# Lead-in of a self-attention: the first pair's queries side by side in both halves, dense products in half steps, fewer filler products

## The reference

```
qkv = x_norm @ W_qkv + b_qkv            # x_norm: layer norm, scaled and shifted
q, k, v = jnp.split(qkv, 3, axis=-1)    # each (B, 1024, 256) -> 16 heads of 16
attn_w = jax.nn.softmax(jnp.einsum('bhqd,bhkd->bhqk', q, k) * scale, axis=-1)
attn_out = jnp.einsum('bhqk,bhkd->bqhd', attn_w, v)
attn_out = attn_out @ W_proj + b_proj
x = x + gate_a[:, None] * attn_out
```

## Time and profile before

| | us |
|---|---|
| median of 3 runs | 1573.97 |
| the runs | 1573.97, 1571.93, 1583.33 |
| the profiled execution | 1573.0 |
| its span | 1571.2 |
| its mean granted PE clock | 0.978 |

### The profile page before, as it was taken

How to read it: one execution, slowest core, us unless ns; L and a number is a source line. 1 busy time by engine, 2 the same in 40 slices (tenths; PEclk the granted TensorE clock), 3 DMA queues, 4 the chain that set the end, 5 groups by cost and what they waited for, 6 DMA issues and landing times.

```text
span 1571.2 us, 26548 instructions
## 1 busy us (share of the span) xinstructions
PE 1452.7 (92%) x10495; PEld 915.3 (58%) x10495; DVE 1052.8 (67%) x2994; ACT 767.8 (49%) x1248; POOL 395.9 (25%) x447
## 2 busy tenths in 40 slices
PE   5889999999999999978998999999999999997898
PEld 3447674344455857656774767444445585765676
DVE  2584356899847446799547544799983754679953
ACT  1335422788844533335552643288884453332554
POOL 4420015642125100113215000664202510001320
PEclk9899998899999999999999999999999999999999
DMA  9500024221020000000040000632102000000000
GB/s 339 174 1 1 0 83 94 42 43 22 2 81 1 1 1 3 2 1 1 1 165 11 1 1 0 165 53 42 22 2 81 1 1 0 3 2 1 1 1 27
DMA packets 41503, 57.86 MB, mean 37 GB/s; under 512 B 10915, under 2 KB 30659, under 8 KB 40603
## 3 DMA queue, kind: packets, MB, share of 16 engines
q1 hardware_dynamic: 25239, 34.71, 6.8%
q0 software_dynamic: 13360, 14.09, 5.1%
q10 hardware_dynamic: 2780, 7.36, 1.3%
HBM read 40.26 MB, written 2.10 MB: 27 GB/s over the span
## 4 chain that ended last, share of the span: by engine, by line
PE 66%; DVE 25%; ACT 4%; issue 2%; DMA 2%; POOL 1%; ACTq 0%; DVEq 0%
PE ps L1039 9%; PE ps L1053 8%; PE ps L488 6%; PE ps L1398 4%; PE ps L898 4%; PE ps L1189 3%; DVE taken L2478 3%; DVE rs L2148 3%; DVE taken L2490 2%; PE ps L876 2%; PE ps L1423 2%; PE ps L1180 2%; PE ps L624 2%; DVE mxw L2140 2%; PE ps L1024 2%
## 5 line engine op out<-in xcount | busy, mean ns | idle before, releaser
L1715 ACT ACTIVATE pt<-ps 128x512 f32<-128x512 f32 x512 | 274.5, 596 | 66.4 <-PE ps L1039 50.7
L2341 DVE TENSOR_REDUCE mm<-ps 128x1 f32<-128x1024 f32 x240 | 288.6, 1222 | 23.3 <-PE ps L1024 20.8
L2596 POOL TENSOR_TENSOR rstd<-ve,minus_half 128x4 f32<-128x4 f32 x32 | 35.0, 1095 | 615.3 <-DVE ve L2012 615.3
L1039 PE MATMUL ps<-qx,kx 50*128 50x512 f32 x512 | 187.8, 457 | 0.8 <-ACT pt L1715 0.8
L1024 PE MATMUL ps<-kx,qx 48*128 48x512 f32 x480 | 180.2, 456 | 1.2 <-DVE mm L2341 1.1
L1053 PE MATMUL ps<-pt,v 128*32 128x256 f32 x2048 | 158.4, 394 | 0.1
L1039 PEld LDWEIGHTS ps<-qx,kx 50*128 50x128 f32 x512 | 79.8, 188 | 88.5 <-ACT pt L1715 69.9
L2225 DVE TENSOR_TENSOR rlo<-ring,rhi 128x512 fp32r<-128x512 f32 x48 | 33.2, 691 | 91.9 <-ACT ring L1667 91.9
L1053 PEld LDWEIGHTS ps<-pt,v 128*32 128x32 f32 x2048 | 44.4, 109 | 84.2 <-ACT pt L1715 56.7
L2643 POOL DMA_DIRECT2D qx<-mxT x64 | 35.9, 563 | 195.7 <-ACT mxT L1709 165.0
L616 PE MATMUL ps<-filler 128*128 128x512 f32 x256 | 83.1, 456 | 0.0
(11 more groups left out here) (378 smaller groups left out, 3380.7 us busy)
## 6 DMA issues: line engine op xcount, KB each, us to landing
wm<-in_L_xcond_W_mlp_dram SPq DMA_DIRECT2D x4, 1024.0 KB, 8.2
w3a<-in_L_xcond_w_m_dram SPq DMA_DIRECT2D x2, 2048.0 KB, 9.0
qx<-q_hi POOLq DMA_DIRECT2D x56, 64.0 KB, 2.3
kx<-k_hi POOLq DMA_DIRECT2D x56, 64.0 KB, 2.3
w<-in_L_xcond_e_w_dram SPq DMA_DIRECT2D x6, 512.0 KB, 7.5
w<-in_L_xcond_e_w_dram SPq DMA_DIRECT2D x2, 1536.0 KB, 13.6
s_ada<-in_L_xcond_w_ada_dram ACTq DMA_DIRECT2D x1, 2304.0 KB, 23.7
w3b<-in_L_xcond_w_m_dram SPq DMA_DIRECT2D x2, 1024.0 KB, 11.3
```

Of the source, the lines that this page charges most:

```text
L1039: pe.matmul(ps[:, bank, :], kx[r, p % 4, kc * P:(kc + 1) * P], qx[r, p % 4, half * 512:(half + 1) * 512], start=True, stop=True).then_inc( ...
L1715: act.activation(pt[:, n % 8, i * 512:(i + 1) * 512], ps[:, bank, :], ACT.Exp, scale=QK_SCALE).then_inc(st_read, 1)
L2341: return dve.tensor_reduce(mm[:, p % 2, e, t:t + 1], place().rearrange("p a q -> p (a q)"), X, ALU.max).then_inc(ring_read, 1)
```

## The change

- Query jobs of pair 0 run side by side (both heads, half of the keys each) for all 16 units, m = 0 to 15, and `maxima` merges both halves of them.
- `values(1)` is dealt out over m = 0 to 5, one half of a tile's accumulation at a time, where it stood in m = 0 to 2 by whole tiles. The dense products follow in half steps at m = 6 to 12, one per unit but two at m = 7, where they stood at m = 3 to 8. The gate products go from m = 10 to m = 11.
- The first block's dense results are read by ACT early (their space is now in block 0 of hT alone), the last two after the gates. The key products' banks start two places later, and `gates` has another place in memory.
- The turn of the first maxima goes from the end of m = 9 to its start, ahead of that unit's query product.
- DVE's `add_v2(1)` goes from after m = 3 to after m = 8.
- Fillers: two at m = 13 and two in each of n = 0 to 3, 10 per batch entry. None stands ahead of n = 0 but those of m = 13.

```diff
 def key_bank(n):
     k = n - TAIL_KEY
-    return 4 + n % 3 if k < 0 else (4 + TAIL_KEY % 3, 4 + (TAIL_KEY + 1) % 3, 4 + (TAIL_KEY + 2) % 3, 1, 3)[k % 5]
+    spare = [4 + (TAIL_KEY + i + 2) % 3 for i in range(3)] + [1, 3]
+    return 4 + (n + 2) % 3 if k < 0 else spare[k % 5]
...
-        gates = at("gates", [P, 3, D], F32, RA + 36 * K1)
+        gates = at("gates", [P, 3, D], F32, RF + 12 * K1)
-        full = [hT[:, qk].rearrange("p c q -> p (c q)") for qk in range(2)]
+        full = [hT[:, :, qk, :] for qk in range(2)]
...
-                    if p == 0 and u < T:
+                    if p == 0:
                         for e in range(2):
-                            r, t, half = slice(64 * e, 64 * e + 3 * HD), u % TB, u // TB
+                            r, t, half = slice(64 * e, 64 * e + 3 * HD), u // T * TB + u % TB, u % T // TB
...
                         if n == 0:
-                            keep_busy(5, 5)
                             pe.wait_ge(gates_ready, b + 1)
+                        elif n == 1:
+                            pe.wait_ge(full_ready, b * 4 + 4)
...
-                    if m == 11:
-                        pe.wait_ge(full_ready, b * 4 + 4)
-                    if m >= 11 and n < 4:
-                        keep_busy(5 if n < 0 else 7, 2 if n < 0 else 1)
...
+                    elif m == 9:
+                        pe.wait_ge(full_ready, b * 4 + 2)
+                        turn_maxima(0, 0)
...
                     query_scores(q, at_m)
-                    if m < TB - 1:
-                        values(1, (m + 1,))
-                    elif m == 3:
+                    left, right = slice(0, 2 * P), slice(2 * P, BLK)
+                    if m < 6:
+                        values(1, (1 + m // 2,), (m % 2,))
+                    elif m == 6:
                         pe.wait_ge(full_ready, b * 4 + 1)
-                        full_step(4, slice(0, 2 * P))
-                    elif m == 4:
-                        full_step(4, slice(2 * P, BLK))
-                        full_step(5, slice(0, 2 * P))
-                    elif m == 5:
-                        full_step(5, slice(2 * P, BLK))
-                    elif m == 6:
+                        full_step(4, left)
+                    elif m == 7:
+                        full_step(4, right)
+                        full_step(5, left)
+                    elif m == 8:
+                        full_step(5, right)
+                    elif m == 9:
+                        pe.wait_ge(st_read, b * N_KEY + 1)
+                        full_step(6, left)
+                    elif m == 10:
+                        full_step(6, right)
+                    elif m == 11:
+                        full_step(7, left)
                         pe.wait_ge(v_ready, b * NB + NB)
-                        full_step(6)
-                    elif m == 7:
-                        full_step(7, slice(0, 2 * P))
-                    elif m == 8:
-                        full_step(7, slice(2 * P, BLK))
-                    elif m == 10:
-                        pe.wait_ge(full_ready, b * 4 + 3)
                         for j in range(3):
...
+                    elif m == 12:
+                        full_step(7, right)
+                    elif m == 13:
+                        pe.wait_ge(full_ready, b * 4 + 3)
                     if n >= 0:
                         key_scores(p, u, 1)
+                    if 13 <= m and n < 4:
+                        keep_busy(7, 2)
...
                 full_part(0, 0, 7)
-                act.wait_ge(full_done, b * 6 + 5)
-                full_part(0, 1, 7)
-                act.wait_ge(full_done, b * 6 + 6)
                 full_part(1, 0, 6)
-                full_part(1, 1, 5)
                 maximum_rows(0)
                 act.wait_ge(gates_spread, b + 1)
...
+                act.wait_ge(full_done, b * 6 + 6)
+                full_part(0, 1, 7)
+                full_part(1, 1, 6)
...
-                        if m == TB - 1:
-                            add_v2(1)
                         if at_m % T == T - 1:
                             maxima(q, at_m // T)
+                        if m == T:
+                            add_v2(1)
```

More of the change, by code:

```diff
@@ L955, in _, with values @@
                         ln(2, 0, bank=2)
-                def values(k, tiles=range(TB)):
+                def values(k, tiles=range(TB), steps=range(KC)):
                     pe.wait_ge(hT_ready, b * 2 * N_HT + 2 * (4 + k + 1))
                     for t in tiles:
-                        for c in range(KC):
+                        for c in steps:
                             ins = pe.matmul(ps[:, 2 + 2 * k + t // 2, t % 2 * D:(t % 2 + 1) * D], hT[:, k, c, t * P:(t + 1) * P],
                                             wv2[:, c, :], start=c == 0, stop=c == KC - 1)
-                    if tiles[-1] == TB - 1:
+                    if tiles[-1] == TB - 1 and steps[-1] == KC - 1:
                         ins.then_inc(v_done, 1)
@@ L977, in full_step @@
                     qk, k, c = j // 2 % 2, j // 4, j % 2
-                    ins = pe.matmul(ps[:, (7, 6, 7, 5)[j // 2], cols], wqk2[:, c, (qk * KC + 1) * P:(qk * KC + 2) * P], hT[:, k, c, cols],
+                    ins = pe.matmul(ps[:, (7, 6, 7, 6)[j // 2], cols], wqk2[:, c, (qk * KC + 1) * P:(qk * KC + 2) * P], hT[:, k, c, cols],
                                     start=c == 0 and cols.start == 0, stop=c == KC - 1 and cols.stop == BLK)
@@ L1118, in _ @@
                         for j in range(3):
                             o = N_ROW * b + R_G_A + j
-                            ins = pe.matmul(ps[:, 7 - j // 2, j % 2 * D:(j % 2 + 1) * D], row_of[:, o:o + 1].broadcast_to([P, P]), row_hl[:, :], start=True, stop=True)
+                            ins = pe.matmul(ps[:, 4 + j // 2, j % 2 * D:(j % 2 + 1) * D], row_of[:, o:o + 1].broadcast_to([P, P]), row_hl[:, :], start=True, stop=True)
                         ins.then_inc(gates_spread, 1)
+                    elif m == 12:
+                        full_step(7, right)
+                    elif m == 13:
+                        pe.wait_ge(full_ready, b * 4 + 3)
@@ L1122, in _ @@
                     if n >= 0:
                         key_scores(p, u, 1)
+                    if 13 <= m and n < 4:
+                        keep_busy(7, 2)
                     for i in bursts_of(n):
                         weigh_values(i // 2, i % 2)
-                    if at_m == 9 and q < NP:
+                    if at_m == 9 and 1 <= q < NP:
                         turn_maxima(q, 0)
@@ L1724, in full_part @@
                     col = (C_BQ2, C_BK2)[qk] + 1
-                    affine(full[qk][:, k * BLK:(k + 1) * BLK], ps[:, bank, :], 1.0, colT[:, col:col + 1]).then_inc(full_ready, 1)
+                    affine(full[qk][:, k, :], ps[:, bank, :], 1.0, colT[:, col:col + 1]).then_inc(full_ready, 1)
                 act.wait_ge(ring_ready, u0 + 1)
@@ L1732, in _ @@
                 full_part(0, 0, 7)
-                act.wait_ge(full_done, b * 6 + 5)
-                full_part(0, 1, 7)
-                act.wait_ge(full_done, b * 6 + 6)
                 full_part(1, 0, 6)
-                full_part(1, 1, 5)
                 maximum_rows(0)
                 act.wait_ge(gates_spread, b + 1)
-                act.activation(gates[:, 0:2, :], ps[:, 7, :].rearrange("p (j n) -> p j n", j=2), ACT.Copy)
-                act.activation(gates[:, 2, :], ps[:, 6, 0:D], ACT.Copy).then_inc(gates_ready, 1)
+                act.activation(gates[:, 0:2, :], ps[:, 4, :].rearrange("p (j n) -> p j n", j=2), ACT.Copy)
+                act.activation(gates[:, 2, :], ps[:, 5, 0:D], ACT.Copy).then_inc(gates_ready, 1)
+                act.wait_ge(full_done, b * 6 + 6)
+                full_part(0, 1, 7)
+                full_part(1, 1, 6)
                 scored = 2
@@ L2336, in query_maximum @@
                 def query_maximum(p, u):
-                    if p == 0 and u < T:
-                        dst = mmq[:, u // TB, :, u % TB]
+                    if p == 0:
+                        dst = mmq[:, u % T // TB, :, u % TB]
                         return dve.tensor_reduce(dst, place(), X, ALU.max).then_inc(ring_read, 1)
@@ L2346, in maxima @@
                     top = mm[:, p % 2, :, half * TB:(half + 1) * TB]
-                    if p == 0 and half == 0:
+                    if p == 0:
                         link(dve.tensor_tensor(top, mmq[:, 0, :, :], mmq[:, 1, :, :], ALU.max))
@@ L2690, in _ @@
                         for qk in range(2):
-                            pool.tensor_copy(dense[2 * qk][:, :], full[qk]).then_inc(hi_ready, 1)
+                            pool.tensor_copy(dense[2 * qk][:, :].rearrange("p (k q) -> p k q", k=NB), full[qk]).then_inc(hi_ready, 1)
                             pool.wait_ge(hi_ready, b * 6 + 4 + qk + 1)
-                            pool.tensor_tensor(dense[2 * qk + 1][:, :], full[qk], dense[2 * qk][:, :].bitcast(F32), ALU.subtract).then_inc(lo_ready, 1)
```

(1 more changed line is left out.)

## The result

| | before | after |
|---|---|---|
| median beside the prediction, us | 1573.46 (4 runs, 1571.93 to 1583.33) | 1557.41 (4 runs, 1556.40 to 1559.79) |
| ratio, 95% interval | | 0.988 [0.9836, 0.9923] |
| profiled execution, its span | 1573.0, 1571.2 | 1556.83, 1555.0 |
| mean granted clock of that execution | 0.978 | 0.985 |
| median with all later runs | 1561.7 (47 runs that held the clock), 1573.4 (45 that did not) | 1556.6 (14 runs, all held) |

What follows compares the result with a forecast made beforehand. PE was taken to bound the kernel. Per entry 2.05 - 0.7 = 1.4 us, 2.8 for both; with entry 0's clock held, 1573.0 - 11.1 - 2.8 = 1559.1, against the median 1560 us, range 1555 to 1573.

Steps and rivals of the forecast that it cites:

- The fall in entry 0: From m = 8 to the turn at n = 11, entry 0 takes 35.99 us against entry 1's 24.90: the clock's fall costs 11.1.
- my likeliest case: In the lead-in, entry 0 holds the clock as entry 1 did: 1559.1, against the median 1560 us; chance 0.45.
- the gap that `add_v2` opens: At m = 9 to 11, DVE's adds hold m = 11 back by 1.28 us; PE has some 2 us idle in 4.2.
- One fall is common: For the kernel before: two of three runs are near the profiled one, which has one fall of the clock.
- the term for n = 0 to 3: Units n = 0 to 3: fillers and side-by-side pairs cost +0.7 us per entry in sum, between 0 and +1.3.
- up to n = 0: Lead-in from m = 0: the first key product goes at 1019.9 to 1020.0 instead of 1022.03, gain 2.05 us.
- within 1%: Whole kernel: chance 0.77 that the time changes by no more than 1%; more than 1% faster is under 1558.2 us.
- 1.37 us of PE time on the path: Ahead of n = 0: the five removed fillers were PE time on the path; DVE stood idle 1.65 us behind them.
- The page of the Trainium skill: For the lead-in's clock: by its rule, taking fillers away would lower the clock and both entries would fall, 1581 us.
- One fall (0.38): Lead-in: one entry still loses the clock, only 2.8 us are won, 1570.2 or 1571; chance 0.38.
- two falls (0.12): At m = 9 to 11, both entries lose the clock, one more fall of 11.1 us: 1581.3 or 1582; chance 0.12.
- no effect (0.05): At n = 0: removed fillers merely uncover another wait, so n = 0 stays where it was, 1573 to 1574; chance 0.05.

Runs made afterwards that it cites:

- the kernel with the adds early: Changed kernel with DVE's two adds of values right after the reduction of m = 6, not after m = 8: median 1581.9 us.
- the later mixed set: A later set of ten runs of the changed kernel beside runs of before, some with the clock held and some not: ratio 0.9932.
- the fillers of the change alone: Kernel before with only its fillers edited: two at m = 13 and two in each of n = 0 to 3, none elsewhere: median 1576.6 us.
- the wait filled with fillers: Changed kernel with DVE's adds after m = 6 and four fillers on PE behind the dense half of m = 8: median 1559.0 us.
- the kernel with whole values: Changed kernel with values(1) in whole tiles at m = 0 to 2, nothing beside the query products of m = 3 to 5: median 1583.5 us.

## Why the prediction was right and wrong

**What bounds, right.** The fall in entry 0 was read as 11.1 us from the earlier trace rows, and 11.07 of the 16.2 us won came from it. Two falls against the change's clock, in the kernel with the adds early, cost (1581.9 - 1556.6) / 2 = 12.7 each, and before's two clusters lie 11.7 apart.

**The mechanism, right, its chance too low.** That dense products beside each query pair would hold the clock was my likeliest case, at 0.45; by their mean clocks none of 14 runs had a fall like before's. The doubt, the gap that `add_v2` opens, was a real danger and in the right place: two reductions sooner it does just that. Where it now stands it is two short waits. I had those two waits at 0.5 and 1.28; they measured 0.34 and 0.98.

**"One fall is common", a step that was too thin.** I took two of three runs near 1573 for the kernel's time. It is one of two times with nearly even odds. Had the four runs of before held the clock, the same change would have shown 0.3%, not 1.0%; beside the later mixed set it showed 0.7%. On which side of 1% the result fell was in part the luck of those four runs.

**The step that failed: the term for n = 0 to 3, +0.7 us per entry.** In entry 0 of the changed kernel PE's products of m = 2 and m = 5, and of n = 0 to 4, started at:

```profile
243.20 0.49 PE L1020 MATMUL ps<-kx,qx 48*128 48x512 f32 x2
...
246.36 0.49 PE L1020 MATMUL ps<-kx,qx 48*128 48x512 f32 x2
...
258.90 0.50 PE L1041 MATMUL ps<-qx,kx 50*128 50x512 f32 x1
...
260.45 0.50 PE L1041 MATMUL ps<-qx,kx 50*128 50x512 f32 x1
...
262.02 0.50 PE L1041 MATMUL ps<-qx,kx 50*128 50x512 f32 x1
...
263.34 0.49 PE L1041 MATMUL ps<-qx,kx 50*128 50x512 f32 x1
...
264.77 0.49 PE L1041 MATMUL ps<-qx,kx 50*128 50x512 f32 x1
```

The four units and the turn took 5.87 us against 5.69, so +0.18 and not +0.7. The two units with a side-by-side pair took 1.55 and 1.57, the third 1.32, the fourth with the turn 1.43, where before a unit took 1.31 to 1.33 from filler to filler: the pair costs about 0.25, not 0.35, and the second filler nothing at the third unit. What lies behind them, to n = 11, took 10.00 against 10.26, so -0.26, where I had nothing: DVE no longer starts late. And up to n = 0 the change took 17.81 against 20.12, a gain of 2.31 where I had 2.05 (m = 0 to 5 at PE's 1.05 a unit and m = 7, which holds two dense halves, at 1.49: 8.97 in all, not 8.7; m = 8 to 13 at 8.84, not 9.4). So the lead-in gave 2.39 per entry where I had 1.4 and an upper end of 2.1. The error, 2.0 us for both entries, carries 1559 over the 1% line to 1557, and with it my 0.77 for "within 1%".

**The fillers.** "1.37 us of PE time on the path" measured as 1.1. The row that spoke for it, 1.65 us of DVE idle ended by PE, was the right one to read.

**The page of the Trainium skill.** By "TensorE: Matmul & The Clock Gate", Part 1, activity releases the half clock. The trace agrees in direction: the fillers of the change alone lost the clock in ten of ten runs, the wait filled with fillers kept it in ten of ten. But no run shows that fewer fillers must lose it, for dense products did the same service; and PE was busy for 27.29 of 27.29 us at 0.50 in the kernel with whole values, so being busy is not by itself enough. Idle time alone does not sort the kernels either: from m = 8 to n = 0 the change is idle for 1.68 of 8.84 us and holds the clock, entry 1 of before for 0.38 of 8.95, and in entry 0 the clock fell with no more than 0.38 us idle in the 5.07 us ahead. Whether it is how much of PE's array the products fill that counts, no run separates.

**Rivals.** One fall (0.38), two falls (0.12) and no effect (0.05) did not come. The two-fall kernel exists, one line away.

## What to carry to other kernels

Before timing a change of 1%, count how often the granted clock falls over several runs of both kernels: two clusters in the times are to be compared each with its like. Where PE waits in a stretch of thin products (query pairs of 48 rows with nothing beside them), it is not the wait's 1 or 2 us that counts but the 11 to 13 that may follow; deal needed dense work into such waits first, and fill with unread products only what is left. Shifting other engines' work by one or two steps can join two harmless waits into a costly one.

## What the runs showed of the hardware

PE at 1.2 GHz (a granted clock of 0.50) can stay there while it is hardly ever idle: for 27.3 us in entry 0 of before (busy for all of them), 41.0 us in the kernel with the change's fillers alone (busy for 40.3), 51.2 us with whole values (busy for 51.1).

The falls were shortest in the kernel that had no fillers at n = 0 to 3, 10.2 and 13.7 us, but not because it came back sooner: they began later, 4.7 and 1.5 us behind n = 0. In all kernels eight of the ten long falls of a lead-in ended 14.9 to 20.5 us behind n = 0, among the bursts of value products (in entry 0 of before the bursts start at 278.4 and the clock rises at 286.8); the other two ended 35.3 and 36.2 us behind it. Nor are bursts needed: entry 1 of the kernel with whole values was back after 3.4 us, at the end of m = 7, after dense products and query pairs. What decides between 3.4 and 51.2 us in the two entries of one execution is open.
